# A lead of twelve units in place of fourteen in the multi-block transformer kernel's global self-attention, with the maxima's rows on SyncE's queue

## The chip, the cores and the metric

The kernel runs on one core of a Trainium2 chip. The metric is the device time of one execution in microseconds (us); lower is better. The core has five engines: PE (TensorE, matmuls), DVE (VectorE), ACT (ScalarE), POOL (GpSimd) and SP (SyncE, which here only issues DMAs). PEld is PE's weight load, which overlaps its matmuls. They wait for one another by semaphores alone.

## The reference

Four transformer blocks run one after another on x of shape (2, 1024, 256): cross attention, a gated mixture of three experts, a block with global self-attention, cross attention and an MLP, and a block with windowed attention, top-k cross attention and a gated MLP. The change lies in the global self-attention of the third block:

```python
x_norm = modulate(_ln(x), shift_a, scale_a)
qkv = x_norm @ W_qkv + b_qkv
q, k, v = jnp.split(qkv, 3, axis=-1)            # 16 heads of 16
attn_w = jax.nn.softmax(jnp.einsum('bhqd,bhkd->bhqk', q, k) * scale, axis=-1)
attn_out = jnp.einsum('bhqk,bhkd->bhqd', attn_w, v)
x = x + gate_a[:, None] * (attn_out @ W_proj + b_proj)
```

Each of the 2 batches has 1024 tokens, 16 heads and full 1024 by 1024 scores, in float32.

## The kernel before

Everything from the weights' set-up to the output is one program; a Python loop writes it out for batch b = 0 and then b = 1, so each part below occurs twice, about 745 us apart. "A pass" is the self-attention of one batch.

**Two streams.** The 16 heads go in 8 pairs p (e = 0, 1 within a pair), and a pair has 16 units u, so a pass has 128 units (`UNITS`). Every unit is worked twice. First, as *query unit* m, PE scores 128 queries against all 1024 keys (`query_scores`, L1020 for the first pair and L1026 after it, two matmuls of 512 columns) into a ring of two PSUM places, and DVE takes each query's maximum over the keys (`query_maximum`, L2354 and L2356). Later, as *key unit* n, PE scores 256 keys against 512 queries (`key_scores`, L1041, two matmuls), with two extra contraction rows that subtract the queries' maxima, ACT takes exp (`probabilities`, L1725, two activations), and some units later PE weighs the values (`weigh_values`, L1057). The loop on L1078 runs n from -LEAD, with m = n + LEAD: in one iteration stand key unit n and query unit m. While n is negative only query units run, with the rest of the projections between them: `values` (L965), `full_step` (L980; it takes bank 6 or 7, and ACT's `full_part` reads its results), and the spreading of three gate rows over the partitions (L1124), which ACT copies into `gates`. The last LEAD key units have no query units beside them and stand in a loop of their own (L1142), two units at a time.

**From maxima to rows.** When the 8 query units of a half of a pair are reduced, DVE combines and splits their maxima (`maxima`, L2363 to L2365), PE turns them (`turn_maxima`, L1033), ACT copies them to `mxT` (`maximum_rows`, L1719) and counts that on `st_read`, and two DMAs of 4 KB each carry them to rows of `qx` (L2656). The first key unit of that half (u = 0 or u = 8) waits for both on `mrow_ld`. The turn stands behind query unit m = 16p + 9 for half 0 and m = 16p + 17 for half 1. In the kernel before the two DMAs are issued on POOL's queue, which also carries the spreads of the next pairs' q and k (`spread`, L2637, six DMAs of 64 KB for each of q and k), the split of the second group of heads, and the multiplication of weights by the gates.

**Start of a pass.** Key unit 0 also waits for `gates`, and key unit 1 for the last `full_part`. Behind query unit 13 and behind key units 0 to 3 two matmuls on a filler tile keep PE going (`keep_busy`, L618). ACT's first exp is preceded by a load of its function table (`ACT_TABLE_LOAD`).

**PSUM.** Query scores use banks 0 to 3, key scores and the turned maxima rotate over banks 4, 5 and 6 (key entry k waits until ACT has read entry k - 3), and bank 7 collects the weighed values. When a pair is complete ACT copies bank 7 to `accS` (L1731), and PE turns it (`finish`, L1067, behind key unit u = 13) for DVE to divide.

Of the kernel before, what the change touches and what calls it, by code (L numbers as in the profile page):

```python
# [19 lines left out]
F32 = mybir.dt.float32  # L20
# [5 lines left out]
P = 128  # L26
D = 256
# [3 lines left out]
T = L // P  # L31
NB = 2
TB = T // NB
BLK = TB * P
H = 16
HD = D // H
# [43 lines left out]
UNITS = H * T  # L80
LEAD = 14
N_RA = 9 * 16
# [5 lines left out]
N_ROW = 8  # L88
# [39 lines left out]
def build(nc, out, g):  # L128
    es = ExitStack()
    with es:  # L130
# [274 lines left out]
        def _(sp):  # L405
# [44 lines left out]
            for b in range(B):  # L450
# [3 lines left out]
                for tile, name in ((wproj, "L2_xcond_W_proj"), (wqc, "L2_xcond_W_qc"), (wcp, "L2_xcond_W_cproj"),  # L454
                                   (wm1, "L2_xcond_W_mlp1"), (wm2, "L2_xcond_W_mlp2"), (wqkv3, "L3_xcond_w_qkv"),
                                   (wso, "L3_xcond_w_so"), (wq3, "L3_xcond_w_q"), (wco, "L3_xcond_w_co")):
                    sp.dma_start(tile[:, :, :], rows(g[name])).then_inc(rc1_ld, 16)

                sp.wait_ge(ring_read, b * N_RING + N_RING)
                sp.wait_ge(pv2_done, b * T * NP + T * NP)  # L460
# [23 lines left out]
        def _(pe):  # L484
# [127 lines left out]
            for b in range(B):  # L612
# [465 lines left out]
                for n in range(-LEAD, TAIL):  # L1078
# [25 lines left out]
                    if m < 6:  # L1104
                        values(1, (1 + m // 2,), (m % 2,))
                    elif m == 6:
                        pe.wait_ge(full_ready, b * 4 + 1)
                        full_step(4, left)
                    elif m == 7:
                        full_step(4, right)  # L1110
                        full_step(5, left)
                    elif m == 8:
                        full_step(5, right)
                    elif m == 9:
                        pe.wait_ge(st_read, b * N_KEY + 1)
                        full_step(6, left)
                    elif m == 10:
                        full_step(6, right)
                    elif m == 11:
                        full_step(7, left)  # L1120
                        pe.wait_ge(v_ready, b * 3 + 2)
                        for j in range(3):
                            o = N_ROW * b + R_G_A + j
                            ins = pe.matmul(ps[:, 4 + j // 2, j % 2 * D:(j % 2 + 1) * D], row_of[:, o:o + 1].broadcast_to([P, P]), row_hl[:, :], start=True, stop=True)  # L1124
                        ins.then_inc(gates_spread, 1)
                    elif m == 12:
                        full_step(7, right)
                    elif m == 13:
                        pe.wait_ge(full_ready, b * 4 + 3)
                    if n >= 0:  # L1130
                        key_scores(p, u, 1)
                    if 13 <= m and n < 4:
                        keep_busy(7, 2)
# [385 lines left out]
        def _(act):  # L1519
# [52 lines left out]
            for b in range(B):  # L1572
# [176 lines left out]
                ins.then_inc(v_ready, 1)  # L1749
                maximum_rows(0)  # L1750
                act.wait_ge(gates_spread, b + 1)
                act.activation(gates[:, 0:2, :], ps[:, 4, :].rearrange("p (j n) -> p j n", j=2), ACT.Copy)
                act.activation(gates[:, 2, :], ps[:, 5, 0:D], ACT.Copy).then_inc(gates_ready, 1)
                act.wait_ge(full_done, b * 6 + 6)
                full_part(0, 1, 7)
# [839 lines left out]
        def _(pool):  # L2595
# [9 lines left out]
            for b in range(B):  # L2605
# [43 lines left out]

                def maximum_rows(p, half):  # L2650

                    pool.wait_ge(st_read, b * N_KEY + key_entries(p, half))
                    pool.sem_inc(passed, 1)
                    for e in range(2):
                        r = 64 * e + 3 * HD
                        pool.dma_start(qx[r:r + 2, p % 4, half * BLK:(half + 1) * BLK].rearrange("r (t c) -> r t c", c=P), mxT[T * e:T * (e + 1), half, :]).then_inc(mrow_ld[half], 16)  # L2656

# [33 lines left out]
                for p in range(NP):  # L2691
                    maximum_rows(p, 0)
                    if p == 0:
# [16 lines left out]
                    elif p + 3 < NP:  # L2710
                        spread(p + 3, (0,))
                    maximum_rows(p, 1)
                    if p == 0:
# [131 lines left out]
```

## Time and profile before

| | |
|---|---|
| median of three runs | 1554.21 us (1552.51 to 1555.72) |
| the profiled execution's own time | 1555.66 us |
| its span, first to last instruction | 1553.8 us |
| mean granted clock of PE | 0.985 of full; 1.00 in both passes |
| busy share PE / DVE / ACT / POOL | 93% / 68% / 50% / 26% |
| first pass, query unit 0 to last exp | 243.1 to 427.6 us |
| second pass, key unit 0 to last exp | 1004.5 to 1172.3 us |

The span is the time between the first and the last instruction that the profiler recorded, and 1.9 us of the profiled execution lie outside it. Busy shares are means over stages with different limits, so the passes are read in their own windows.

### The profile page before, as it was taken

The numbers are of one execution on the slowest core, as the hardware profiler recorded it, in microseconds if no ns is written. First come the engines' busy times: TensorE is split into PE (matmuls) and PEld (weight loads), VectorE is DVE, ScalarE is ACT, GpSimd is POOL, SyncE is SP. The second block draws the span as 40 slices with busy tenths as digits, with TensorE's granted clock in tenths as the row PEclk, the third lists the DMA queues.
The fourth block names the chain that finished last, engine by engine and source line by source line (L and its number), as shares of the span: only waits on it lengthen the run. The fifth ranks groups of instructions, "written<-read, shape, count | busy, mean of one in ns | idle before, by whom it ended". The sixth has DMA issues, their size and how long they took to land.

```text
span 1553.8 us, 26548 instructions
## 1 busy us (share of the span) xinstructions
PE 1438.2 (93%) x10489; PEld 909.9 (59%) x10489; DVE 1050.1 (68%) x2992; ACT 769.3 (50%) x1252; POOL 400.4 (26%) x449
## 2 busy tenths in 40 slices
PE   5889999999989999978998999999999999998898
PEld 3447674344456757656765767434445585765676
DVE  2584358999657346899457534799974744679953
ACT  1335424888833533325543542388883453333554
POOL 4330018641053010114133000764213411011320
PEclk9999999999999999999999999999999999999999
DMA  9600015220020000000140000622102000000000
GB/s 336 183 1 1 0 66 123 43 43 13 2 82 1 1 1 3 1 1 1 45 132 1 1 0 14 165 44 42 22 3 82 1 1 1 3 2 1 1 1 27
DMA packets 41503, 57.86 MB, mean 37 GB/s; under 512 B 10915, under 2 KB 30659, under 8 KB 40603
## 3 DMA queue, kind: packets, MB, share of 16 engines
q1 hardware_dynamic: 25239, 34.71, 6.8%
q0 software_dynamic: 13360, 14.09, 5.1%
q10 hardware_dynamic: 2780, 7.36, 1.4%
q8 instruction: 83, 1.36, 0.4%
q14 instruction: 41, 0.34, 0.1%
HBM read 40.26 MB, written 2.10 MB: 27 GB/s over the span
## 4 chain that ended last, share of the span: by engine, by line
PE 65%; DVE 25%; ACT 4%; issue 2%; DMA 2%; POOL 1%; ACTq 0%; DVEq 0%
PE ps L1041 8%; PE ps L1057 8%; PE ps L490 6%; PE ps L1408 4%; PE ps L900 4%; PE ps L1199 3%; DVE taken L2491 3%; DVE rs L2163 3%; PE ps L878 2%; PE ps L1433 2%; PE ps L1190 2%; DVE taken L2503 2%; PE ps L626 2%; DVE mm L2356 2%; DVE mxw L2155 2%
## 5 line engine op out<-in xcount | busy, mean ns | idle before, releaser
L1725 ACT ACTIVATE pt<-ps 128x512 f32<-128x512 f32 x512 | 273.8, 595 | 48.0 <-PE ps L1041 32.6
L2356 DVE TENSOR_REDUCE mm<-ps 128x1 f32<-128x1024 f32 x224 | 269.0, 1222 | 8.5 <-PE ps L1026 6.3
L2609 POOL TENSOR_TENSOR rstd<-ve,minus_half 128x4 f32<-128x4 f32 x32 | 35.0, 1094 | 614.3 <-DVE ve L2027 614.3
L1041 PE MATMUL ps<-qx,kx 50*128 50x512 f32 x512 | 182.3, 447 | 0.9 <-ACT pt L1725 0.8
L1026 PE MATMUL ps<-kx,qx 48*128 48x512 f32 x448 | 163.2, 444 | 0.7 <-DVE mm L2356 0.3
L1057 PE MATMUL ps<-pt,v 128*32 128x256 f32 x2048 | 156.2, 389 | 0.1
L1041 PEld LDWEIGHTS ps<-qx,kx 50*128 50x128 f32 x512 | 77.7, 184 | 88.9 <-ACT pt L1725 70.6
L2240 DVE TENSOR_TENSOR rlo<-ring,rhi 128x512 fp32r<-128x512 f32 x48 | 33.2, 691 | 91.8 <-ACT ring L1677 91.8
L1057 PEld LDWEIGHTS ps<-pt,v 128*32 128x32 f32 x2048 | 44.1, 108 | 83.0 <-ACT pt L1725 57.5
L2656 POOL DMA_DIRECT2D qx<-mxT x64 | 35.9, 564 | 174.0 <-ACT mxT L1719 148.8
L618 PE MATMUL ps<-filler 128*128 128x512 f32 x246 | 77.1, 447 | 0.7 <-ACT hT L1521 0.7
L2116 DVE TENSOR_TENSOR x<-x,ps 128x512 f32<-128x512 f32 x64 | 41.7, 683 | 51.0 <-PE ps L642 27.5
L1026 PEld LDWEIGHTS ps<-kx,qx 48*128 48x128 f32 x448 | 65.9, 184 | 5.5 <-DVE mm L2356 5.0
L1677 ACT ACTIVATE rhi<-ps,mod 128x512 fp32r<-128x512 f32 x48 | 33.2, 691 | 69.0 <-PE ps L810 68.9
L2446 DVE TENSOR_REDUCE mxw<-ps 128x8 f32<-128x1024 f32 x32 | 38.8, 1224 | 39.2 <-PE ps L1260 39.2
L2767 POOL TENSOR_TENSOR prob<-prob,m 128x1024 f32<-128x1024 f32 x16 | 31.0, 1937 | 123.1 <-DVE taken L2491 123.1
L2155 DVE TENSOR_REDUCE mxw<-ps 128x16 f32<-128x1024 f32 x32 | 37.7, 1220 | 34.7 <-PE ps L676 34.7
L1833 ACT ACTIVATE wprobT<-ps 128x1024 f32<-128x1024 f32 x32 | 32.8, 1024 | 56.6 <-PE ps L1286 56.2
L2163 DVE RECIPROCAL rs<-ps 128x512 f32<-128x512 f32 x16 | 53.7, 3356 | 7.3 <-PE ps L713 7.3
L2034 DVE TENSOR_SCALAR xhat<-x,mv,rstd 128x256 f32<-128x256 f32 x128 | 46.4, 425 | 17.6 <-POOL rstd L2609 17.5
L618 PEld LDWEIGHTS ps<-filler 128*128 128x128 f32 x246 | 46.9, 201 | 17.1 <-issue 8.3
L1521 ACT ACTIVATE hT<-ps,mod 128x512 f32<-128x512 f32 x48 | 34.7, 777 | 38.5 <-PE ps L626 38.5
(380 smaller groups left out, 3420.1 us busy)
## 6 DMA issues: line engine op xcount, KB each, us to landing
wm<-in_L_xcond_W_mlp_dram SPq DMA_DIRECT2D x4, 1024.0 KB, 8.7
w3a<-in_L_xcond_w_m_dram SPq DMA_DIRECT2D x2, 2048.0 KB, 8.4
qx<-q_hi POOLq DMA_DIRECT2D x56, 64.0 KB, 2.3
kx<-k_hi POOLq DMA_DIRECT2D x56, 64.0 KB, 2.3
w<-in_L_xcond_e_w_dram SPq DMA_DIRECT2D x6, 512.0 KB, 6.9
w<-in_L_xcond_e_w_dram SPq DMA_DIRECT2D x2, 1536.0 KB, 13.6
s_ada<-in_L_xcond_w_ada_dram ACTq DMA_DIRECT2D x1, 2304.0 KB, 24.4
w3b<-in_L_xcond_w_m_dram SPq DMA_DIRECT2D x2, 1024.0 KB, 10.9
```

What stands on the lines that cost most here:

```text
L490: ins = pe.matmul(ps[:, bank, :], w[:, c, m * P:(m + 1) * P], src[:, c, :], start=c == 0, stop=c == KC - 1)
L618: pe.matmul(ps[:, bank, :], filler[:, 0:P], filler[:, :], start=True, stop=True)
L900: ins = pe.matmul(ps[:, 6 - 2 * (j % 2) + c, :], w_[:, m, c * P:(c + 1) * P], part, start=n % 4 == 0 and i == 0, stop=n % 4 == 3 and i == 2)
L1026: ins = pe.matmul(ps[:, bank + half, :], qx[r, p % 4, t * P:(t + 1) * P], kx[r, p % 4, half * 512:(half + 1) * 512], start=True, stop=True)
L1041: pe.matmul(ps[:, bank, :], kx[r, p % 4, kc * P:(kc + 1) * P], qx[r, p % 4, half * 512:(half + 1) * 512], start=True, stop=True).then_inc( ...
L1057: ins = pe.matmul(ps[o:o + 32, 7, half * 2 * P:(half + 1) * 2 * P], v2[:, kc, VS * (2 * p + e):VS * (2 * p + e) + 32], weights[:, :, part, ...
L1199: ins = pe.matmul(ps[:, 4 + 2 * k + j, :], w2s[:, wp, m, j * P:(j + 1) * P], gelus[sp][:, m % 4, :], start=m == 0 and (wp, sp) == (0, 0), ...
L1408: ins = pe.matmul(ps[:, 4 + i, :], w3ap[wp][:, c, (NC_HID * i + m) * P:(NC_HID * i + m + 1) * P], src[:, c, :], start=(wp, part, c) == (0, ...
L1725: act.activation(pt[:, n % 8, i * 512:(i + 1) * 512], ps[:, bank, :], ACT.Exp, scale=QK_SCALE).then_inc(st_read, 1)
L2155: ins = dve.tensor_reduce(mxw[:, t, :].rearrange("p (r n) -> p r n", r=4)[:, :, 0:4], ps[:, bank:bank + 4, o:o + D].rearrange("p r (h s) - ...
L2163: link(dve.reciprocal(rs2[:, u % 2, :], ps[:, bank + 1, :]))
L2356: return dve.tensor_reduce(mm[:, p % 2, e, t:t + 1], place().rearrange("p a q -> p (a q)"), X, ALU.max).then_inc(ring_read, 1)
```

## The change

Four edits. `LEAD` is 12, so the key stream starts two query units earlier, each turn of maxima stands two key units nearer to the key unit that uses it, and twelve units, not fourteen, stand in the last loop. SP's program gets the two row DMAs of each half, behind the loads of the next weights; POOL's `follow_maxima` keeps the wait for `st_read` and drops the DMAs. On PE the projections' steps are packed into fewer query units: `full_step` 4 and 5 whole at m = 6 and 7, the gates' three matmuls at m = 8, `full_step` 6 and 7 in halves at m = 9 to 11, and the filler behind m = 13 goes. ACT copies the gates ahead of the first maxima, not behind them.

```diff
-LEAD = 14
+LEAD = 12
...
+                for p in range(NP):
+                    for half in range(2):
+                        sp.wait_ge(st_read, b * N_KEY + key_entries(p, half))
+                        for e in range(2):
+                            r = 64 * e + 3 * HD
+                            sp.dma_start(qx[r:r + 2, p % 4, half * BLK:(half + 1) * BLK].rearrange("r (t c) -> r t c", c=P).bitcast(F32), mxT[T * e:T * (e + 1), half, :].bitcast(F32)).then_inc(mrow_ld[half], 16)
                 sp.wait_ge(ring_read, b * N_RING + N_RING)
...
                     elif m == 6:
                         pe.wait_ge(full_ready, b * 4 + 1)
-                        full_step(4, left)
+                        full_step(4)
                     elif m == 7:
-                        full_step(4, right)
-                        full_step(5, left)
+                        full_step(5)
                     elif m == 8:
-                        full_step(5, right)
+                        pe.wait_ge(v_ready, b * 3 + 2)
+                        for j in range(3):
+                            o = N_ROW * b + R_G_A + j
+                            ins = pe.matmul(ps[:, 4 + j // 2, j % 2 * D:(j % 2 + 1) * D], row_of[:, o:o + 1].broadcast_to([P, P]), row_hl[:, :], start=True, stop=True)
+                        ins.then_inc(gates_spread, 1)
                     elif m == 9:
                         pe.wait_ge(st_read, b * N_KEY + 1)
                         full_step(6, left)
                     elif m == 10:
                         full_step(6, right)
+                        full_step(7, left)
                     elif m == 11:
-                        full_step(7, left)
-                        pe.wait_ge(v_ready, b * 3 + 2)
-                        for j in range(3):
-                            o = N_ROW * b + R_G_A + j
-                            ins = pe.matmul(ps[:, 4 + j // 2, j % 2 * D:(j % 2 + 1) * D], row_of[:, o:o + 1].broadcast_to([P, P]), row_hl[:, :], start=True, stop=True)
-                        ins.then_inc(gates_spread, 1)
-                    elif m == 12:
                         full_step(7, right)
-                    elif m == 13:
-                        pe.wait_ge(full_ready, b * 4 + 3)
                     if n >= 0:
                         key_scores(p, u, 1)
-                    if 13 <= m and n < 4:
+                    if n == 0:
+                        pe.wait_ge(full_ready, b * 4 + 3)
+                    if 0 <= n < 4:
                         keep_busy(7, 2)
...
-                maximum_rows(0)
                 act.wait_ge(gates_spread, b + 1)
                 act.activation(gates[:, 0:2, :], ps[:, 4, :].rearrange("p (j n) -> p j n", j=2), ACT.Copy)
                 act.activation(gates[:, 2, :], ps[:, 5, 0:D], ACT.Copy).then_inc(gates_ready, 1)
+                maximum_rows(0)
...
-                def maximum_rows(p, half):
+                def follow_maxima(p, half):
 
                     pool.wait_ge(st_read, b * N_KEY + key_entries(p, half))
                     pool.sem_inc(passed, 1)
-                    for e in range(2):
-                        r = 64 * e + 3 * HD
-                        pool.dma_start(qx[r:r + 2, p % 4, half * BLK:(half + 1) * BLK].rearrange("r (t c) -> r t c", c=P), mxT[T * e:T * (e + 1), half, :]).then_inc(mrow_ld[half], 16)
```

The first place is PE's order at the start of a pass, from the turn of the first maxima to the first key unit. Before:

```order
L1033 MATMUL ps<-ident,mhl 16x128 [waits mt_ready,full_ready]
L1020 MATMUL ps<-kx,qx 128x512 [waits ring_read]
L1020 MATMUL ps<-kx,qx 128x512
L980 MATMUL ps<-hT,wqk_99 128x256 [waits st_read]
L1020 MATMUL ps<-kx,qx 128x512 [waits ring_read]
L1020 MATMUL ps<-kx,qx 128x512
L980 MATMUL ps<-hT,wqk_99 128x256
L1020 MATMUL ps<-kx,qx 128x512 [waits ring_read]
L1020 MATMUL ps<-kx,qx 128x512
L980 MATMUL ps<-hT,wqk_99 128x256
L1124 MATMUL ps<-row_hl,row_of 128x256 [waits v_ready]
L1124 MATMUL ps<-row_hl,row_of 128x256 x2
```

And now (L1039 is the turn, L1026 a query unit, L986 a `full_step`, L1047 the key scores):

```order
L1039 MATMUL ps<-ident,mhl 16x128 [waits mt_ready,full_ready]
L1026 MATMUL ps<-kx,qx 128x512 [waits ring_read]
L1026 MATMUL ps<-kx,qx 128x512
L986 MATMUL ps<-hT,wqk_99 128x256 [waits st_read]
L1026 MATMUL ps<-kx,qx 128x512 [waits ring_read]
L1026 MATMUL ps<-kx,qx 128x512
L986 MATMUL ps<-hT,wqk_99 128x256 x2
L1026 MATMUL ps<-kx,qx 128x512 [waits ring_read]
L1026 MATMUL ps<-kx,qx 128x512
L986 MATMUL ps<-hT,wqk_99 128x256
L1047 MATMUL ps<-qx,kx 128x512 [waits mrow_ld0,gates_ready]
L1026 MATMUL ps<-kx,qx 128x512 [waits ring_read]
```

Behind the turn stood four query units, a fifth, the gates and a filler ahead of the first key unit; now three query units stand there, and the gates have moved ahead of the turn.

The second place is PE's order in the middle of a pass, around the turn of half 0 of a later pair. Before, its first four units behind the turn begin with:

```order
L1033 MATMUL ps<-ident,mhl 16x128 [waits mt_ready,st_read]
L1041 MATMUL ps<-qx,kx 128x512 [waits st_read]
L1026 MATMUL ps<-kx,qx 128x512 [waits ring_read]
L1026 MATMUL ps<-kx,qx 128x512
L1041 MATMUL ps<-qx,kx 128x512 [waits st_read]
```

and there are four such units, with the turn of the accumulator (L1067) behind the second, until the key score that waits for `mrow_ld0`. Now (L1073 is the turn of the accumulator, L1063 the weighing of values):

```order
L1039 MATMUL ps<-ident,mhl 16x128 [waits mt_ready,st_read]
L1073 MATMUL ps<-ident,accS 128x128 [waits acc_read,ring_read]
L1073 MATMUL ps<-ident,accS 128x128 x3
L1047 MATMUL ps<-qx,kx 128x512 [waits st_read]
L1032 MATMUL ps<-kx,qx 128x512 [waits ring_read]
L1032 MATMUL ps<-kx,qx 128x512
L1047 MATMUL ps<-qx,kx 128x512 [waits st_read]
L1063 MATMUL ps<-pt,v_188 32x256 [waits st_read]
L1063 MATMUL ps<-pt,v_188 32x256 x3
L1047 MATMUL ps<-qx,kx 128x512 [waits st_read]
```

This second unit is the last one ahead of the key score with the wait for `mrow_ld0`: two units are left where there were four.

The third place is ACT's order at the start of a pass. Before:

```order
L1747 ACTIVATE v_188<-ps 128x2x16x16 x2
L1719 ACTIVATE mxT<-ps 16x128
L1752 ACTIVATE gates<-ps 128x512
L1753 ACTIVATE gates<-ps 128x256
L1521 ACTIVATE hT<-ps,colT 128x512 x2
```

And now:

```order
L1750 ACTIVATE v_188<-ps 128x2x16x16 x2
L1754 ACTIVATE gates<-ps 128x512
L1755 ACTIVATE gates<-ps 128x256
L1722 ACTIVATE mxT<-ps 16x128
L1524 ACTIVATE hT<-ps,colT 128x512 x2
```

The first copy of maxima stands behind the two copies of the gates.

## Rows read from the trace of the kernel before

**Rows 1.** Busy time by window: us, each engine's busy time (instructions), clock, DMA.

```profile
320.00:341.33 21.33, 21.33 (x202) 8.75 (x198) 20.52 (x24) 18.00 (x36) 9.49 (x18) 1.00 0.24 40
```

**Rows 2.** Timeline, start of the first pass, ACT: start us, us, instruction [idle before].

```profile
253.88 0.27 ACT L1719 ACTIVATE mxT<-ps 16x128 fp32r<-16x128 f32 x1 [3.25 <-PE ps L1033]
...
257.41 0.60 ACT L1752 ACTIVATE gates<-ps 128x512 f32<-128x512 f32 x1 [3.26 <-PE ps L1124]
...
258.47 1.27 ACT L1521 ACTIVATE hT<-ps,colT 128x512 f32<-128x512 f32 x2 [0.19 <-PE ps L980]
259.76 1.28 ACT L1725 ACT_TABLE_LOAD   x1
261.05 2.07 ACT L1725 ACTIVATE pt<-ps 128x512 f32<-128x512 f32 x4
```

**Rows 3.** Timeline, the same stretch, PE.

```profile
253.58 0.27 PE L1033 MATMUL ps<-ident,mhl 128*16 128x128 f32 x1 [0.36 <-DVE mhl L2365]
...
256.67 0.70 PE L1124 MATMUL ps<-row_hl,row_of 128*128 128x256 f32 x3
...
257.31 0.50 PE L1020 MATMUL ps<-kx,qx 48*128 48x512 f32 x2
...
257.74 0.70 PE L980 MATMUL ps<-hT,wqk 128*128 128x256 f32 x2
...
259.88 0.50 PE L1041 MATMUL ps<-qx,kx 50*128 50x512 f32 x1
...
263.00 0.50 PE L1041 MATMUL ps<-qx,kx 50*128 50x512 f32 x1
```

**Rows 4.** Timeline, the same stretch, DVE.

```profile
260.65 1.23 DVE L2354 TENSOR_REDUCE mmq<-ps 128x2 f32<-128x1024 f32 x1 [0.43 <-PE ps L1020]
262.20 1.23 DVE L2354 TENSOR_REDUCE mmq<-ps 128x2 f32<-128x1024 f32 x1 [0.32 <-PE ps L1020]
...
264.44 3.48 DVE L2356 TENSOR_REDUCE mm<-ps 128x1 f32<-128x1024 f32 x3
```

**Rows 5.** Timeline, turn for half 1 of pair 5, PE.

```profile
371.66 0.28 PE L1033 MATMUL ps<-ident,mhl 128*16 128x128 f32 x1
...
374.24 0.49 PE L1041 MATMUL ps<-qx,kx 50*128 50x512 f32 x1
...
375.47 0.49 PE L1041 MATMUL ps<-qx,kx 50*128 50x512 f32 x1
...
377.13 0.50 PE L1041 MATMUL ps<-qx,kx 50*128 50x512 f32 x1
```

**Rows 6.** Timeline, up to the first key unit of pair 7, PE.

```profile
406.04 0.66 PE L1067 MATMUL ps<-ident,accS 128*128 128x128 f32 x4
...
409.32 0.50 PE L1041 MATMUL ps<-qx,kx 50*128 50x512 f32 x1
```

**Rows 7.** Timeline, last loop of the first pass, PE and ACT.

```profile
411.79 1.31 PE L1041 MATMUL ps<-qx,kx 50*128 50x512 f32 x4
...
414.34 0.27 ACT L1719 ACTIVATE mxT<-ps 16x128 fp32r<-16x128 f32 x1
...
415.00 3.93 ACT L1725 ACTIVATE pt<-ps 128x512 f32<-128x512 f32 x8
...
419.40 8.19 ACT L1725 ACTIVATE pt<-ps 128x512 f32<-128x512 f32 x16 [0.47 <-PE ps L1041]
```

**Rows 8.** Source view of L2656, the rows' DMAs: issue to landing.

```profile
DMA to landing us min/median/max: 1.6/1.7/3.4
```

**Rows 9.** DMA issues: size of one, median us to landing.

```profile
qx<-q_lo POOLq DMA_DIRECT2D x28, 64.0 KB, 2.2
...
out_dram<-x SPq DMA_DIRECT2D x4, 64.0 KB, 2.4
```

**Rows 10.** Timeline, end of the first pass, DVE and SP's queue.

```profile
430.48 0.49 DVE L2372 TENSOR_TENSOR xhat<-ps,fr 128x128 f32<-128x128 f32 x2
...
430.99 0.37 SPq L461 DMA_DIRECT2D w3a<-in_L_xcond_w_m_dram  x1
```

More of the change, by code:

```diff
@@ L2691, in _ @@
                 for p in range(NP):
-                    maximum_rows(p, 0)
+                    follow_maxima(p, 0)
                     if p == 0:
@@ L2711, in _ @@
                         spread(p + 3, (0,))
-                    maximum_rows(p, 1)
+                    follow_maxima(p, 1)
                     if p == 0:
```

## Prediction

> **What bounds the kernel now.** I first looked at busy time by window. In a middle stretch of sixteen units PE is busy for all 21.33 us, with DVE at 20.52 and ACT at 18.00 [rows 1]. The middle of a pass is thus PE's, 1.33 us a unit on average and 1.23 for a plain one (374.24 to 375.47) [rows 5], with DVE close behind. PE's clock is 1.00 there, so the clock is no term. A change of the lead alters no work, only which units stand side by side; what it can gain or lose lies in three places, and I read the timelines of those: the start of a pass, the waits for the maxima's rows, and the last loop. Everything outside the passes is untouched.
>
> At the start the reader sees a chain: PE's last `full_step` at 257.74 [rows 3], ACT's two `full_part`s at 258.47, the table load at 259.76, the first exp at 261.05 [rows 2]. Beside it DVE reduces query units 14 and 15 at 260.65 and 262.20, when PE brings them with key units 0 and 1, and unit 16 at 264.44 [rows 4]. In the last loop there are no query units, and ACT sets the pace: sixteen exps in 8.19 us, so 1.02 us a unit, after an idle 0.47 [rows 7].
>
> **The change, part by part** (for one pass; there are two).
>
> *Start.* Between the turn at 253.58 and the last `full_step`, PE loses the gates (256.67 to 257.31, 0.64 us) and one query unit (257.31 to 257.74, 0.43) [rows 3]. Against that the first `mxT` copy now stands behind the gates' copies. Their matmuls would end near 253.2, when the two copies (both fit between 257.41 and 258.47, so under 1.1 us [rows 2]) begin, so `mxT` starts some 0.2 us later than 253.88, and the next `full_step` waits for it. That is 0.9 us earlier; I take 1.1, since the fuller units also fill short gaps in which PE waited for DVE. The chain moves as one: first exp at 259.95. The second score of key unit 1 needs a bank that this exp frees (0.6 us later), and a filler and a gap follow (1.0), so key unit 2 starts at 261.5, not 263.0 [rows 3].
>
> That gain of 1.5 isn't kept. Query units 12 to 15 now ride with key units 0 to 3, and those wait for ACT. Query unit 14 comes with key unit 2, and DVE gets it 0.77 later (259.88 to 260.65 [rows 3, 4]), at 262.3; unit 15 is 1.55 later (260.65 to 262.20), and unit 16, behind the maxima, 2.24 after that (262.20 to 264.44), at 266.1, not 264.44 [rows 4]. Query unit 18 needs the place that unit 16 frees. So the query stream is 1.7 us later than before; the key stream, two units nearer, is 2 x 1.23 - 1.7 = 0.8 us earlier. From here on the two are tied. **-0.8.** The filler pair that goes lay in this stretch.
>
> *Rows by SP.* From a turn to rows in place: copy starts 0.30 later and takes 0.27 [rows 2, 3]; SP picks up a finished count in 0.02 (430.97 to 430.99 [rows 10]); its first issue takes 0.37, so the second begins some 0.42 later; then the landing, L. Together 1.01 + L. No row shows a 4 KB transfer on SP. POOL's take 1.7 [rows 8], its 64 KB ones 2.2, and SP's 64 KB ones 2.4 [rows 9]: subtracting POOL's difference gives 1.9, which I take. The bounds are 1.6, POOL's fastest [rows 8], and 2.4 [rows 9].
>
> What is left to hide it: for half 1, the turn (0.2) and two units (374.24 to 377.13), 3.1 us; before it was 5.5 (371.66 to 377.13) [rows 5]. For half 0 of a later pair, the turn and 406.04 to 409.32, 3.5 us [rows 6]. For half 0 of pair 1, where no accumulator is turned, 0.2 + 2 x 1.23 = 2.65. With L = 1.9 the chain is 2.9: hidden by 0.2 and 0.6, and late by 0.25 once. With 2.4 it is 3.4: half 1 late by 0.3 seven times and pair 1 by 0.75, 3.0 in all. **+0.25 (0 to 3.0).** PE is the bound here, and behind its waiting key score stand the query scores that DVE needs, so a wait counts in full. POOL loses two issues of 0.56 a half and only its spreads stand behind them; nobody waits for those. SP's waits stand ahead of the loads of `w3a`, which are issued after the pass anyway.
>
> *Last loop.* Before, from its first key score to the last exp, 411.79 to 427.59, 15.8 us [rows 7]. Two units fewer are 2 x 1.02 = 2.05 less; the same two units now stand in the middle, +2.46. The turn for the last half is now followed by two units, not four, until its rows are used. ACT works on those for 1.97 (half of the 3.93 at 415.00), while the rows take 0.02 + 0.42 + 1.9 = 2.34 from the copy's end, and score to exp 0.5: idle for 0.87 where it was 0.47 [rows 7] (0.57 with L = 1.6, 1.37 with 2.4). 2.46 - 2.05 + 0.40 = **+0.8 (0.5 to 1.3).**
>
> *Sum.* -0.8 + 0.25 + 0.8 = +0.25 a pass, **+0.5 us in all.** With L = 1.6: -0.8 + 0 + 0.5, -0.6 in all; with 2.4: -0.8 + 3.0 + 1.3, +7. The sum was made against the profiled execution, 1555.66 us, which is 1.4 above the median of the runs; set on the median, 1554.21, it gives 1554.7.
>
> The rows show 1.7 us for POOL's small transfers. The Trainium skill ("DMA: Bandwidth & Descriptors", "Anatomy of one DMA") gives a fixed cost of about 2.0 us to a DMA from this kind of queue, which the trace undercuts; by 2.0 on SP the sum would be about +1 in all. The same page ("Specifications") has the hardware queue's first byte 0.4 us ahead of the software queue's; by 1.3 the sum would be an estimated -0.8. No row of this case tells which holds for SP.
>
> **The rivals.**
>
> *Late landings are no longer absorbed (slower).* One of POOL's transfers took 3.4 us [rows 8]. With 5.5 us to hide in [rows 5] that cost next to nothing; with 3.1 a landing of 3.4 stalls PE by 1.01 + 3.4 - 3.1 = 1.3. From three such in the 32 halves on, the kernel is slower by over 0.2%: three give +3.9, with the sum 1558.6. For it: the slack falls to 0.2. Against: the median is 1.7, and SP may not share the cause. The Trainium skill says of a transfer on SP's queue that only as many of the 16 DMA engines take part as divide both sides' outer dimensions, here 2, where POOL's waits for all 16 ("DMA: Bandwidth & Descriptors", "Why a DMA increments its semaphore by 16 and not by 1"). By that late ones would be an eighth as frequent, and the time the 1554.7 above. No run here shows it yet.
>
> *SP's small transfers take as long as its large ones (slower).* L = 2.4: 1561. It passes 0.2% from about 2.15 on, where half 1 begins to wait in every pair. For it: SP's 64 KB rows. Against: POOL's landings fall with size.
>
> *The start's gain is kept (faster side).* If DVE's queue doesn't hold the key stream, the 1.5 us of key unit 2 stay, and with L = 1.6 a pass is -1.5 + 0 + 0.5 = -1.0: 1552.2. Against: DVE has 0.8 us of slack in 21.33, too little to catch up 0.7 at once.
>
> **How the numbers follow.** 0.2% is 3.1 us, about what a measurement of this kernel can tell from no change. The sum as worked out: 0.56, in 1552.7 to 1556.5. Start kept: 0.16, and with a little more somewhere half of that passes -3.1. Late landings: 0.17, mostly over +3.1. L near 2.4: 0.11. Faster 0.10, within 0.2% 0.65, slower 0.25. The range of 8 in 10 runs from 1551.3, which leaves out the outer part of the third rival, to 1559.6, which leaves out L = 2.4.
>
> **What would show it.** First exp 1.1 us earlier after the start of the query stream, DVE's unit 16 about 1.7 us later. SP's row transfers landing in 1.6 to 2.2 us, the second issue 0.4 behind the first. PE's wait for them at the first key unit of pair 1, few or none elsewhere. The last loop 13.8 to 14.4 us from first key score to last exp. The prediction is wrong if PE waits for rows in most halves (slower), or if the key stream enters the middle of the pass over 1.5 us early (faster).

## The result and the profile after

The changed kernel takes 1572.9 us in the median of four runs (1569.2 to 1576.1), beside 1554.97 for the kernel before in the same series. The ratio is 1.0113, 95% interval 1.0101 to 1.0126: slower by 18 us, where 1554.7 was forecast and the range ended at 1559.6. The profiled execution took 1573.76 us with a span of 1572.0; its mean granted clock is 0.976, not 0.985.

**Where the 18.2 us of span went.** I measured both passes in both traces from PE's first query unit (L1020 before, L1026 after) to the end of the last exp. Before: 243.11 to 427.59 and 987.74 to 1172.30, so 184.5 and 184.6 us. After: 244.35 to 435.71 and 995.87 to 1190.33, so 191.4 and 194.5. That is +6.9 and +9.9. Another 1.2 lies ahead of the first pass, which the change doesn't touch, and the stretch between the passes is 560.15 us in both. The loss is inside the passes.

**Where in the pass.** Windows of the first pass of the kernel after (us, busy time and instructions of PE, PEld, DVE, ACT, POOL, then the granted clock, DMA share, GB/s):

```profile
255.00:260.00 5.00, 4.47 (x19) 2.30 (x18) 4.36 (x4) 1.67 (x5) 3.66 (x8) 1.00 0.44 73
260.00:265.00 5.00, 4.20 (x14) 1.93 (x13) 2.88 (x3) 4.30 (x8) 4.33 (x6) 0.85 0.47 86
265.00:270.00 5.00, 5.00 (x14) 2.75 (x15) 2.54 (x5) 2.19 (x4) 0.00 (x0) 0.50 0.00 0
270.00:275.00 5.00, 5.00 (x27) 1.90 (x27) 3.58 (x3) 3.03 (x7) 1.76 (x4) 0.50 0.10 16
275.00:280.00 5.00, 5.00 (x46) 1.69 (x44) 3.09 (x3) 3.05 (x6) 4.07 (x9) 0.78 0.78 142
...
325.00:346.33 21.33, 21.20 (x202) 8.65 (x198) 20.28 (x24) 17.88 (x35) 7.09 (x13) 1.00 0.22 40
```

The granted clock is the column that matters: 0.50, the lower of its two levels (1.2 GHz), from 263.5 to 277.2 in this pass and from 1014.4 to 1031.5 in the second, 13.7 and 17.1 us. The kernel before has no such stretch in either pass; outside the passes both kernels have some (from 552.3 to 555.7 in the kernel before, for one), so its mean is 0.985 and not 1.00. PE is busy for all 5.00 us in the rows at 0.50, but a key score of 512 columns takes 709 ns on average between 266 and 276, and 449 ns from 325 on: a busy share of 100% there is a slow engine, not a full one. DVE, which stands close behind PE in [rows 1], is busy for 2.54 and 3.58 of 5.00 us in these two rows, ACT for 2.19 and 3.03. From 325 on the clock is 1.00 and the row is that of [rows 1] but for 0.13 us of PE.

**What PE did before the clock fell.** Timeline of the kernel after, PE, which answers to [rows 3]:

```profile
255.81 0.70 PE L986 MATMUL ps<-hT,wqk 128*128 128x256 f32 x2 [0.32 <-ACT mxT L1722]
...
259.26 0.47 PE L1047 MATMUL ps<-qx,kx 50*128 50x512 f32 x1 [0.21 <-DMA qx<-mxT]
...
260.78 0.50 PE L1047 MATMUL ps<-qx,kx 50*128 50x512 f32 x1
260.79 0.73 PE L1026 MATMUL ps<-kx,qx 48*128 48x512 f32 x2
262.32 0.49 PE L1047 MATMUL ps<-qx,kx 50*128 50x512 f32 x1 [0.80 <-ACT pt L1728]
...
263.40 1.13 PE L1026 MATMUL ps<-kx,qx 48*128 48x512 f32 x2
```

and ACT in the same stretch, which answers to [rows 2]:

```profile
254.75 0.60 ACT L1754 ACTIVATE gates<-ps 128x512 f32<-128x512 f32 x1 [2.88 <-PE ps L1121]
...
255.51 0.25 ACT L1722 ACTIVATE mxT<-ps 16x128 fp32r<-16x128 f32 x1
259.09 1.27 ACT L1524 ACTIVATE hT<-ps,colT 128x512 f32<-128x512 f32 x2 [3.33 <-PE ps L986]
260.37 1.28 ACT L1728 ACT_TABLE_LOAD   x1
261.67 0.60 ACT L1728 ACTIVATE pt<-ps 128x512 f32<-128x512 f32 x1
```

The second score of key unit 1 needs the bank that the first exp frees. PE is there at 261.52, and the exp, behind two full parts and its table load, ends at 262.3: 0.80 us of idle. In the kernel before, one query unit (13) and a filler pair more stood between the last `full_step` and this score, and PE came to it (262.01) after the exp had freed the bank. Its only idle of the stretch was ahead of that filler pair, for ACT's full part:

```profile
259.21 0.74 PE L618 MATMUL ps<-filler 128*128 128x512 f32 x2 [0.35 <-ACT hT L1521]
```

In the changed kernel, with the 0.21 for the rows PE has idled 1.01 us in the 5 us before the fall. The second pass repeats it (0.18 and 0.84). The last row is the fall itself: two matmuls in 1.13 us, where the same two took 0.73 at 260.79.

DVE, which answers to [rows 4], gets its query units late in consequence; the first row is unit 14, the second begins with unit 16:

```profile
264.58 1.23 DVE L2357 TENSOR_REDUCE mmq<-ps 128x2 f32<-128x1024 f32 x1 [1.79 <-PE ps L1026]
...
270.02 2.36 DVE L2359 TENSOR_REDUCE mm<-ps 128x1 f32<-128x1024 f32 x2 [0.89 <-PE ps L1032]
```

Counted from the first query unit, unit 16 comes at 25.7 us; forecast was 23.0 (266.1 less 243.1).

**The rest of the change did what was forecast, or nearly.** Last loop of the first pass, ACT, which answers to [rows 7]:

```profile
424.43 2.00 ACT L1728 ACTIVATE pt<-ps 128x512 f32<-128x512 f32 x4
427.51 8.20 ACT L1728 ACTIVATE pt<-ps 128x512 f32<-128x512 f32 x16 [1.08 <-PE ps L1047]
```

From its first key score (421.60) to the last exp's end it takes 14.1 us, forecast 13.8 to 14.4. In the second pass 3.4 us at clock 0.50 stand in that loop too, and it takes 15.55. For the rows' DMAs, which answer to [rows 8], the source view of L464 gives no landing times on SP's queue, but issue times and waits:

```profile
L464 SPq DMA_DIRECT2D qx<-mxT x64: 610/610/772, 255.8 to 1178.4; - x64
...
  PEld ps L1047: 9.2, 16
  PE ps L1047: 1.5, 6
```

PE waited for rows six times, 1.5 us in the whole program. The place that the prediction named is the first key unit of pair 1:

```profile
284.74 0.28 PE L1039 MATMUL ps<-ident,mhl 128*16 128x128 f32 x1
...
285.06 0.27 ACT L1722 ACTIVATE mxT<-ps 16x128 fp32r<-16x128 f32 x1
...
285.35 1.26 SPq L464 DMA_DIRECT2D qx<-mxT  x2
...
287.79 0.49 PE L1047 MATMUL ps<-qx,kx 50*128 50x512 f32 x1 [0.30 <-DMA qx<-mxT]
```

The turn for half 1 of pair 5, which answers to [rows 5], shows how little is left to hide the rows in, as forecast (3.1 us):

```profile
381.24 0.28 PE L1039 MATMUL ps<-ident,mhl 128*16 128x128 f32 x1
...
384.37 0.50 PE L1047 MATMUL ps<-qx,kx 50*128 50x512 f32 x1
```

Back at pair 1, 1.26 us for two issues of 0.61 puts the second at 286.00. PE resumes at 287.79, and in the traces with rows by POOL it does so 0.04 behind a landing, so L is 1.75 us.

### The profile page after: what moved, and what is told of

Its sections match the earlier page's. It is cut to its first block, busy times and chain, and to the rows that moved or that the text cites. A ratio compares the mean times of both kernels' runs of the same rounds, so it can differ in the third digit from the quotient of the medians.

```text
span 1572.0 us, 26524 instructions
## 1 busy us (share of the span) xinstructions
PE 1451.1 (92%) x10477; PEld 909.3 (58%) x10477; DVE 1050.0 (67%) x2992; ACT 770.7 (49%) x1252; POOL 363.9 (23%) x385
## 4 chain that ended last, share of the span: by engine, by line
PE 65%; DVE 22%; ACT 6%; issue 2%; DMA 2%; SPq 2%; POOL 1%; DVEq 0%; ACTq 0%
PE ps L1047 9%; PE ps L1063 8%; PE ps L496 6%; PE ps L1411 4%; PE ps L906 4%; PE ps L1202 3%; DVE taken L2494 3%; DVE rs L2166 3%; DVE taken L2506 2%; PE ps L884 2%; PE ps L1436 2%; PE ps L1193 2%; PE ps L632 2%; DVE mxw L2158 2%; PE ps L1263 2%
## 5 line engine op out<-in xcount | busy, mean ns | idle before, releaser
L1047 PE MATMUL ps<-qx,kx 50*128 50x512 f32 x512 | 192.3, 463 | 3.8 <-ACT pt L1728 1.6
L1032 PE MATMUL ps<-kx,qx 48*128 48x512 f32 x448 | 167.0, 454 | 0.0
L1063 PE MATMUL ps<-pt,v 128*32 128x256 f32 x2048 | 162.0, 402 | 0.1
L1047 PEld LDWEIGHTS ps<-qx,kx 50*128 50x128 f32 x512 | 80.3, 190 | 104.8 <-ACT pt L1728 78.6
L1063 PEld LDWEIGHTS ps<-pt,v 128*32 128x32 f32 x2048 | 45.0, 110 | 86.2 <-ACT pt L1728 56.8
L2640 POOL DMA_DIRECT2D qx<-q_hi x72 | 35.2, 496 | 91.8 <-ACT pt L1728 47.7
## 6 DMA issues: line engine op xcount, KB each, us to landing
w<-in_L_xcond_e_w_dram SPq DMA_DIRECT2D x2, 1536.0 KB, 13.7
```

The source lines that it names most:

```text
L1032: ins = pe.matmul(ps[:, bank + half, :], qx[r, p % 4, t * P:(t + 1) * P], kx[r, p % 4, half * 512:(half + 1) * 512], start=True, stop=True)
L1047: pe.matmul(ps[:, bank, :], kx[r, p % 4, kc * P:(kc + 1) * P], qx[r, p % 4, half * 512:(half + 1) * 512], start=True, stop=True).then_inc( ...
L1063: ins = pe.matmul(ps[o:o + 32, 7, half * 2 * P:(half + 1) * 2 * P], v2[:, kc, VS * (2 * p + e):VS * (2 * p + e) + 32], weights[:, :, part, ...
```

## The experiments

**Theory C (clock).** The change leaves PE idle around the first key units; the grant falls to 1.2 GHz in both passes, and that is the loss. **Theory R (rows).** The rows come late from SP's queue. **Theory L (lead).** The shorter lead or its packing costs the time by itself. Times below are medians beside runs of the kernel before on the same chip.

**1. A filler pair where PE idled.** On the changed kernel:

```diff
+                    if n == 1:
+                        keep_busy(7, 2)
                     if n >= 0:
                         key_scores(p, u, 1)
```

> The changed kernel with one filler pair more, ahead of key unit 1's second score, where PE idled 0.80 us in the first pass and 0.84 us in the second just before its granted clock fell to 0.50. Theory C (the clock: the change leaves PE idle at the start of a pass, the grant falls to 1.2 GHz for 13.7 us in the first pass and 17.1 us in the second, and that costs about 7 and 10 us): the idle falls from 1.93 to about 1.2 us, and if it was this idle that decided, no window at 0.50 stands inside a pass, pair 0 takes about 21.5 us and the time is 1555 to 1558. Theory R (the rows' transfers on SP's queue come late, and PE waits for them): nothing changes but 0.0 to 0.7 us of added work, so 1572 to 1574. Theory L (the shorter lead in itself, by the way it packs the queues): 1572 as well.

Measured: 1558.7 us, before 1554.7, ratio 1.0033 (1.0021 to 1.0045), just above the range that C gave. Two matmuls more a pass, and some 14 us less. PE and the clock (timeline, then windows):

```profile
259.12 0.74 PE L624 MATMUL ps<-filler 128*128 128x512 f32 x2
260.02 0.49 PE L1047 MATMUL ps<-qx,kx 50*128 50x512 f32 x1 [0.16 <-ACT pt L1730]
```

```profile
257.50:262.50 5.00, 4.84 (x18) 2.15 (x16) 3.06 (x3) 4.76 (x8) 4.55 (x6) 1.00 0.52 93
262.50:267.50 5.00, 5.00 (x33) 2.55 (x35) 4.57 (x8) 3.89 (x9) 0.00 (x0) 1.00 0.00 0
```

The wait is 0.16 and the clock stays at 1.00. In the second row PE runs 20 matmuls of 512 columns and 13 short ones; the changed kernel ran 14 of 512 columns and none of the short ones in its row from 265 on. ACT's first exp comes as late as in the changed kernel (17.3 us after the first query unit), so it isn't an earlier chain that helps. The passes take 185.9 and 187.5 us (the second with 3.4 us at clock 0.50 in its last loop). Against the changed kernel's that prices the falls at 5.4 and 7.0 us, the filler pair paid. R and L are refuted as the main cause: neither the queue nor the lead was touched.

**2. The lead alone.** The kernel before with `LEAD = 12`.

> The kernel before with LEAD = 12 alone: rows by POOL, the steps of the projections at their old query units, gates behind the first maxima, the fillers at key units 1 to 3. Theory C: the last full step now stands beside key unit 0 and key unit 1 waits for both of ACT's full parts, some 1.3 us, and then for the first exp; more idle than in the changed kernel, so the clock falls in both passes and the time is 1572 to 1580. Theory R: rows are on POOL's queue and land in 1.7 us, so 1555 to 1558. Theory L: 1572 without any window at half clock inside a pass.

**3. The queue alone.** The kernel before with the rows' DMAs in SP's program and out of POOL's, as in the change.

> The kernel before with the rows' DMAs on SP's queue alone, LEAD 14 and everything else as it was. Theory C: the rows have 5.5 us to hide in and PE's idle at the start stays 0.7 us, so no clock fall and 1554 to 1556. Theory R: if SP's transfers take 5 us or more, or disturb the other transfers, PE waits at most halves and the time is 1560 to 1572.

**4. All but the queue.** The changed kernel with the two DMAs back in POOL's program, behind `pool.sem_inc(passed, 1)`.

> The changed kernel with the rows' DMAs back on POOL's queue, LEAD 12 and the new packing kept. Theory C: the waits for mxT and for the first exp, 0.32 and 0.80 us, stand as they were, so the clock falls as in the changed kernel: 1569 to 1574, or up to 1 us less where POOL's rows land sooner. Theory R: the time comes back to 1555 to 1558.

Measured: lead alone 1590.8 us (ratio 1.0234, 1.0201 to 1.0267); queue alone 1554.4 (1.0003, 0.9991 to 1.0015); all but the queue 1589.3 (1.0221, 1.0197 to 1.0244). The queue by itself is harmless, and the other two lose their clock in both passes, as C has it. But they came out 11 and 15 us above the upper ends that C gave. In both the profiled execution is the fastest of four, 5.7 and 4.3 us below the median, so its passes show only part of that. Part is PE's wait for rows. In the changed kernel with POOL's rows the source view of L2653 says

```profile
L2653 POOL DMA_DIRECT2D qx<-mxT x64: 537/556/621, 255.3 to 1191.2; - x64
...
  PEld ps L1041: 26.3, 26
  PE ps L1041: 13.8, 18
...
DMA to landing us min/median/max: 1.6/1.7/2.7
```

and around the same key unit of pair 1

```profile
283.53 0.28 PE L1033 MATMUL ps<-ident,mhl 128*16 128x128 f32 x1
...
284.81 1.13 POOL L2653 DMA_DIRECT2D qx<-mxT  x2 [5.63 <-ACT mxT L1716]
...
287.13 0.49 PE L1041 MATMUL ps<-qx,kx 50*128 50x512 f32 x1 [0.86 <-DMA qx<-mxT]
```

The landings are as fast as SP's (1.7 and 1.75 us), but POOL starts 0.70 us after `mxT` is there and SP 0.02. From the turn to rows in place it is 3.6 us by POOL and 3.0 by SP, and the lead of 12 leaves 2.65 to 3.5. So PE waits 13.8 us in 18 places, not 1.5 in six (with the lead alone, 11.6 us in 18), and from key unit 16 to the last loop the passes take 4.4 and 7.2 us longer than the changed kernel's. The 7.2 hold one half whose rows POOL issued 2.16 us behind its maxima: PE waited 2.47 us for them, and behind that wait stands a stretch of 3.4 us at 0.50 that the first pass doesn't have. Why the other executions of these two versions take longer still, at mean clocks of 0.969 to 0.974, was not looked at in a trace. At this lead the move to SP's queue is worth 16 us of the median (1589.3 against 1572.9); at a lead of 14 it is worth nothing that the median shows. The late landings of the first rival exist on POOL (four of 32 halves at 2.4 to 2.7); on SP every wait for rows from pair 1 on, but for the last loop's, ended within 3.6 us of its turn.

**5. The idle taken away, not filled.** A rival is left, theory P: the clock falls by what the whole stretch does, and the filler helped only as added matmuls. One exp of 16 values on ACT behind its copy of the maxima, in ACT's 3.3 us of idle, so that the table is loaded there (`warm` is a tile of 16 values that nothing reads):

```diff
+        warm = keep("warm", [2 * T, 1])
...
                 maximum_rows(0)
+                act.activation(warm[:, :], ident[0:2 * T, 0:1], ACT.Exp, scale=QK_SCALE)
                 act.wait_ge(full_done, b * 6 + 6)
```

> The changed kernel with one exp of 16 single values on ACT between its copy of the first maxima and its first full part, so that the table load of 1.28 us falls into ACT's idle 3.3 us there and no longer stands ahead of the first exp. No filler is added. Theory C (PE's idle before key unit 1's second score lets the granted clock fall): the first exp starts 1.28 us earlier, some 16.0 us after the first query unit and not 17.3; the 0.80 us of idle is gone, no window at 0.50 stands inside the first pass, and the time is that of the version with the filler pair less up to 0.7 us a pass: 1556 to 1559. Theory P (the clock falls by what the whole stretch draws or does, and a filler helped only as added matmuls): the clock falls as in the changed kernel, 1569 to 1573.

Measured: 1555.1 us, before 1555.6, ratio 1.0002 (0.9994 to 1.0011). The first exp starts at 15.9 us, key unit 1 waits for nothing, the clock holds in both passes (184.8 and 185.0 us), and the loss is gone without one matmul added. Theory P falls. ACT, then the window in which the changed kernel stood at 0.50:

```profile
255.13 1.28 ACT L1758 ACT_TABLE_LOAD   x1
256.42 0.20 ACT L1758 ACTIVATE warm<-ident 16x1 f32<-16x1 f32 x1
```

```profile
265.00:270.00 5.00, 5.00 (x49) 2.28 (x47) 4.90 (x8) 4.35 (x9) 1.88 (x4) 1.00 0.15 22
```

**6. The same early exp in the kernel before.** There I put it at the same statement, ahead of the full parts, which in that kernel is behind the gates' copies.

> The kernel before with the same early exp of 16 values. Theory C: the clock is kept either way, the first exp starts 1.28 us earlier, and PE, which ran fillers there, gains 0 to 0.7 us a pass: 1553 to 1555. If the start of the key stream were kept to the end, as one rival of the prediction had it: 1552.

Measured: 1571.4 us, ratio 1.0104 (1.0091 to 1.0117), a clear miss. ACT, and PE's row behind it:

```profile
257.57 0.38 ACT L1754 ACTIVATE gates<-ps 128x256 f32<-128x256 f32 x1
257.97 1.28 ACT L1755 ACT_TABLE_LOAD   x1
259.26 0.20 ACT L1755 ACTIVATE warm<-ident 16x1 f32<-16x1 f32 x1
259.37 1.23 ACT L1522 ACTIVATE hT<-ps,colT 128x512 f32<-128x512 f32 x2
```

```profile
260.09 0.73 PE L619 MATMUL ps<-filler 128*128 128x512 f32 x2 [1.55 <-ACT hT L1522]
```

The load came ahead of the full parts and not in idle time; PE idled 1.55 us in place of 0.35, and the clock fell for 17.1 us in both passes (in the second, for 3.4 in the last loop too). The lead, the queue and the packing are those of the kernel before here, and the time is that of the changed one.

**7. The same, in the right place**, directly behind the maxima's copy and ahead of the wait for the gates.

> The kernel before with the early exp right behind ACT's copy of the first maxima, where ACT is idle for 3.3 us, and not behind the gates' copies as in the earlier run, where its table load held back the full parts and PE idled 1.55 us. Theory C: PE's idle there is 0.35 us as in the kernel before, the clock is kept, the fillers fill the pass's start as they did, and the time is that of before: 1554 to 1556. If it is the early exp itself that harms: 1570.

Measured: 1555.0 us, ratio 1.0000 (0.9990 to 1.0009). With experiment 6 this is one instruction moved by two places on ACT: 16 us.

**8. The kernel before without its fillers**, and **9. the changed kernel with `LEAD = 14`.**

> The kernel before without its five filler pairs, behind query unit 13 and behind key units 0 to 3; LEAD 14, rows by POOL. Theory C: PE then idles for the table load and the first exps, 1 to 3 us in place of 0.35; the clock falls in both passes and the time is 1568 to 1575 without any change of the lead. Rival (the lead of 12 is the cause, and the clock falls with it for other reasons): the fillers are but added work, and the time is 1552 to 1555.

> The changed kernel with LEAD = 14: the new packing, the gates first, the rows by SP and four filler pairs, but two query units more ahead of the first key unit. Theory C: two more query units cover the full parts and the table load in part, but the pair behind query unit 13 is gone; the idle before the first exps lies between the kernel before's 0.35 and the changed one's 1.3 us, so the clock is kept or falls in one pass: 1552 to 1556, 1562 at the most. Theory L (the new packing is the cause and not the lead): 1569 to 1573.

Measured: 1562.2 us (1.0043, 1.0029 to 1.0056) and 1560.8 (1.0037, 1.0025 to 1.0049). Both lose the clock for 13.7 us in each pass, 8 as C said, 9 against its better case. In number 8 PE comes to the second score of key unit 1 before the first exp is done, and the fall comes inside that wait, 0.54 and 0.89 us into it:

```profile
261.75 1.28 PE L1041 MATMUL ps<-qx,kx 50*128 50x512 f32 x2 [0.92 <-ACT pt L1723]
```

It is 6 us cheaper than the lower end that I gave. Ten matmuls a pass are gone from it, which fits, but their share was not measured by itself. Number 9 shows where its idle comes from: at a lead of 14 the packed start leaves two bare query units in a row, and PE waits for DVE:

```profile
257.05 0.50 PE L1026 MATMUL ps<-kx,qx 48*128 48x512 f32 x2 [0.27 <-DVE mmq L2357]
...
258.18 0.50 PE L1026 MATMUL ps<-kx,qx 48*128 48x512 f32 x2 [0.41 <-DVE mmq L2357]
```

So either half of the change on PE, the lead (experiment 2) or the packing without the filler behind query unit 13, loses the clock alone.

**10 and 11. How many fillers are needed.** The version of experiment 5 with `keep_busy(7, 1)`, and without the call.

> The version with the early exp (LEAD 12, rows by SP, new packing) with one filler matmul behind each of key units 0 to 3 in place of two. With the table load out of the way those four units take 1.55 us each, where DVE needs 1.23 for its reduction, so four fillers of 0.32 us are added work and nothing more. Theory C: 1.2 us less a pass, no window at 0.50 at the start, 1552 to 1554. Rival (the fillers are what keeps the grant, whatever the idle): the clock falls and the time is 1565 to 1572.

> The same without any filler behind key units 0 to 3. PE's work in such a unit is then about 0.9 us against DVE's 1.23, so PE idles some 0.3 us a unit, 1.2 in all. Theory C: that idle is as large as in the versions that lost the clock; the grant falls to 0.50 in both passes and the time is 1562 to 1570, though less is done. Rival (the clock does not depend on this idle): 1551 to 1553.

Measured: one filler a unit 1555.1 us (1.0012, 0.9994 to 1.0030); none 1561.5 (1.0035, 1.0023 to 1.0046). Without fillers PE waits 0.16 us for rows and 0.31 for a full part in the first pass, and the clock falls, for 10.2 and 6.8 us. That idle is 0.5 us a pass, not the 1.2 that I gave, and still the clock fell; the time is just under the range. With one each key unit 16 comes 1.0 us earlier, where 1.2 was worked out, and the profiled passes are 185.0 (3.4 us at clock 0.50 in its last loop) and 184.0. But the median does not move: its twelve runs reach from 1553.2 to 1566.0, and the longest two have the lowest mean clocks, 0.980 and 0.979 where the others have 0.982 to 0.985.

**12. The best of all parts.** The kernel before with SP's rows, the early exp in the right place and one filler matmul in place of two.

> The kernel before (LEAD 14, old packing) with the rows by SP, the early exp behind the first maxima and one filler matmul in place of two behind query unit 13 and key units 0 to 3. Theory C: no idle of over 0.4 us at the start, the clock is kept, and each pass is some 0.7 (SP's rows) and 1.2 to 1.5 (five fillers less) shorter: 1551 to 1553, the fastest of all. Rival: idle comes in place of the fillers and the clock falls, 1565 to 1570.

Measured: 1557.3 us, ratio 1.0021 (1.0001 to 1.0041), range 1553.7 to 1570.5; 1551 to 1553 was forecast, a miss. The profiled execution has the shortest passes of all, 182.9 and 183.2 us, at clock 1.00. Yet eight of the twelve runs have a mean clock of 0.981 or less and take 1557 to 1570. No version that I tried beats the kernel before by more than the noise; the lowest ratio is 1.0000.

**All of them by idle and clock.** Pass 1 / pass 2. Idle is the sum of PE's gaps of 0.1 us and more in the timeline from 13 us after the first query unit to the fall, or to 20 us after it where the clock held. Between 10 and 12 us after it every version has idle of 0.3 to 0.4 us, which is left out.

| version | idle, us | at 0.50 there, us | pass, us | median, us |
|---|---|---|---|---|
| 10 | 0.11 / 0.12 | none | 185.0 / 184.0 | 1555.1 |
| 5 | 0.18 / 0.22 | none | 184.8 / 185.0 | 1555.1 |
| before | 0.35 / 0.35 | none | 184.5 / 184.6 | 1554.97 |
| 7 | 0.35 / 0.35 | none | 184.4 / 184.5 | 1555.0 |
| 3 | 0.35 / 0.35 | none | 183.8 / 183.9 | 1554.4 |
| 12 | 0.35 / 0.35 | none | 182.9 / 183.2 | 1557.3 |
| 1 | 0.35 / 0.38 | none | 185.9 / 187.5 | 1558.7 |
| 11 | 0.47 / 0.52 | 10.2 / 6.8 | 188.5 / 185.3 | 1561.5 |
| 9 | 0.67 / 0.67 | 13.7 / 13.7 | 188.9 / 189.0 | 1560.8 |
| 8 | 0.89 / 1.24 | 13.7 / 13.7 | 188.0 / 188.1 | 1562.2 |
| after | 1.01 / 1.02 | 13.7 / 17.1 | 191.4 / 194.5 | 1572.9 |
| 4 | 1.04 / 1.03 | 13.7 / 13.7 | 197.5 / 200.5 | 1589.3 |
| 6 | 1.55 / 1.55 | 17.1 / 17.1 | 192.5 / 194.2 | 1571.4 |
| 2 | 2.12 / 1.89 | 17.1 / 17.1 | 199.8 / 200.0 | 1590.8 |

Every pass whose start kept the clock has less idle there than any that lost it. The lengths of some passes also hold a stretch of 3.4 us at 0.50 further on: the second of 1, 4, 6 and of the changed kernel, and the first of 10 and 11. All this is so in the profiled executions; the mean clocks of versions 10 and 12 show that others of the same kernel can lose more.

## Why the prediction was wrong

**The step that failed** stands in its first paragraph: "PE's clock is 1.00 there, so the clock is no term." The row was read rightly, but it lies in the middle of a pass, and it is a row of the kernel before. At the start of the pass the change takes away a query unit and a filler pair that stood between PE's last `full_step` and the second score of key unit 1. I costed the fillers as work saved, "the filler pair that goes lay in this stretch", and the wait of key unit 1's second score as a delay in a chain. Experiments 1, 5, 6 and 7 show what such a wait is besides: it set the clock of the next 13.7 and 17.1 us. That term, which the sum put at nothing, is 14 to 18 us: the changed kernel's median is 14.2 above that of experiment 1, which pays for fillers, and 17.8 above that of experiment 5, in which the early exp also brings key unit 16 forward by 1.0 to 1.1 us a pass against experiment 1.

The Trainium skill ("TensorE: Matmul & The Clock Gate", "A second HAM failure mode: psum-queue depth-cycling") describes a kernel whose clock goes up and down because PE idles shortly and often while it cycles through PSUM banks. The table agrees as to the short gaps: none that it counts is over 1.6 us, and in experiment 11 the fall followed gaps of 0.16 and 0.31. It does not show the up and down: at the start of a pass the clock fell once. The Trainium skill ("TensorE: Matmul & The Clock Gate", "Terms") prices a fall at half of the time spent at the half rate, an estimated 6.8 us for 13.7 and 8.5 for 17.1; the runs show 5.4 and 7.0 between experiment 1 and the changed kernel. With the measured stretches put to my sum, that price of the Trainium skill gives an estimated 1554.7 + 6.8 + 8.5 = 1570.

**The start, -0.8 a pass.** First exp 1.1 us earlier was the forecast; it was 0.6 (17.94 to 17.32 us after the first query unit). The wait for `mxT` came as foreseen (0.32); not foreseen was that key unit 0 waits for its rows (0.21). The -0.8 itself can't be read from the changed kernel, whose key unit 16 came 5.5 and 7.0 us late. With the clock kept it came 0.1 us late in experiment 1, extra fillers included, and 0.9 early in experiment 5, early exp included.

**Rows by SP, +0.25.** L is 1.75 us (1.9 taken, 1.6 to 2.4 as bounds), the second issue 0.65 behind the first (0.42 taken): 3.0 in place of 2.9, and right by errors that cancel. Half 0 of pair 1 waited 0.30 and 0.29 (forecast 0.25); not foreseen were 0.22 and 0.26 for half 1 of pair 1, beside those of key unit 0. From key unit 16 to the last loop, experiment 1 takes 133.8 us where the kernel before takes 130.8 for two units fewer: +3.0, beside 2.46 + 0.25.

**Last loop, +0.8.** Measured 14.1 us at full clock, and ACT's idle 1.08, not 0.87. The term held.

**The sum.** Between experiments 7 and 5, both with an early exp and the clock kept, a pass grows by 0.3 and 0.6 us; forecast was 0.25. Without the clock the forecast of no change would have held.

**The rivals.** Late landings, L of 2.4 and a kept start: none occurred in the changed kernel, as far as PE's waits show it. All three shared the premise that failed, so none could catch it.

## What to carry to other kernels

A wait of PE has two prices: its own length, and what the clock does after it; ask for each matmul or filler that a change takes out of a thin stretch which engine PE will wait for there, and look at the granted clock of the stretch behind. Prefer taking the wait away to filling it: a function table loaded in an idle stretch of ACT gave back as much as fillers did, and more. And where a chain's slack is cut, compare the queues by the time from the finished count to the first issue, since the landings of both were the same.

## What the runs showed of the hardware

**Two queues, one landing time.** A 4 KB transfer from SBUF to SBUF takes 1.7 us to land from POOL's queue (median of the trace) and 1.75 from SP's (worked out above from PE's wait at pair 1, since SP's landings are not recorded). SP starts 0.02 us after the count and needs 0.61 an issue; POOL mostly starts 0.70 after it and needs 0.56.

**DVE stands still for a POOL instruction.** The queue alone (experiment 3) shortened each pass by 0.7 us, though PE never waited for rows in the kernel before. DVE's split of the maxima for half 1 of pair 0 in the kernel before, and POOL at that time:

```profile
284.29 1.03 DVE L2364 CAST mhl<-mm 128x8 fp32r<-128x8 f32 x1
```

```profile
282.88 2.40 POOL L2709 TENSOR_TENSOR k_lo<-hT,k_hi 128x1024 fp32r<-128x1024 f32 x1
```

and the same in experiment 3:

```profile
282.22 0.17 DVE L2370 CAST mhl<-mm 128x8 fp32r<-128x8 f32 x1
```

```profile
279.45 2.40 POOL L2712 TENSOR_TENSOR k_lo<-hT,k_hi 128x1024 fp32r<-128x1024 f32 x1
```

Eight values a partition take 1.03 us and end 0.04 after POOL's instruction ends (285.28), or 0.17 where POOL is done by then; DVE's reductions from PSUM beside POOL keep their 1.23. The cast takes 1.03 in both passes of the kernel before and 1.00 and 1.02 in experiment 7, and under 0.3 in 3, 9 and 12, which have their rows by SP. Counted from the pass's first query unit, which in experiment 3 came 1.9 us earlier in the trace, POOL's split comes 1.5 us earlier without the rows' DMAs and the cast 0.2, so the split ends ahead of it. The Trainium skill ("SBUF — State Buffer", "Who interferes with whom") says that a cast can take the port pair that DVE shares with GpSimd, and that who comes second is blocked for the other's whole instruction, while a reduction never is. These rows agree. That the 0.86 us at this place make up the pass's 0.7 was not tried by itself; 0.2 of the 0.7 were gained ahead of key unit 16, which starts before this cast.

**Open.** The table sorts the versions by their idle, but not the length of the fall: 1.02 us gave 17.1 in one pass and 1.24 gave 13.7 in another. Less idle also means more matmuls done in the same stretch, and no run separates the two: that the wait cost the clock is shown, but not what in it the clock follows. Nor is it settled why versions with fewer fillers, whose profiled executions kept the clock, lose some of it in others. And in the last loop single stretches of 3.4 us at clock 0.50 come and go between executions, at 1.2 to 1.6 us each.
